# Retention scores contracted in two halves of 64 rows, into two PSUM banks, with spread queries of half the size

## The chip, the cores and the metric

One core of one Trainium2 chip runs the kernel. The time is that of one execution on the device in microseconds, the median of three runs. Before the change it is 919.24 us (918.93 to 920.19).

## The reference, cut to what matters

The program takes x of 4 batches, 1024 positions and 128 channels, normalizes it, and adds two branches to it: a block with retention, and a network of two layers of local attention (8 heads of 64, windows of 64) with a gated feed-forward part. The change concerns the retention alone. It has 16 heads of 8 channels, and a decay for each head:

```python
q = l2_normalize(xn @ qw.T)
k = l2_normalize(xn @ kw.T)
v = xn @ vw.T
dmask = jnp.where(causal[None], gammas[:, None, None] ** exponent[None], 0.0)
sim = jnp.einsum('bhnd,bhmd->bhnm', qh, kh) * scale
sim = sim * dmask[None]
yh = jnp.einsum('bhnm,bhmd->bhnd', sim, vh)
```

## The kernel before, in words

All tensors are fp32, but for a small mask. Positions are worked on in 8 tiles of 128 for all 4 batches. Each engine has a program of its own, written out in the order in which it issues; semaphores hold the engines together, and no planner moves anything. `run_bodies` goes through 16 steps of the attention (8 tiles by 2 layers); each step has four slots, one for each batch. In the eight steps of the first layer, a stage of retention for the same tile follows the last slot: `pe_retention`, `dve_retention` and `pool_retention`, each with the four batches as blocks b = 0 to 3. So there are 8 such stages and 32 blocks, and they lie in the first half of the execution.

Inside a block the 128 positions are 4 chunks (c, NBL) of 32. The decays are put on the queries and keys (aqk), so that the mask of a chunk's scores is only causal. The 128 channels are 16 heads of 8; a head is 4 g + j, with a group g (0 to 3, 32 channels each) and a place j in the group. The queries are spread over the groups: `qx` (in the memory of `prT`) holds for each chunk four copies of the turned queries, copy g with all channels but those of group g set to zero (`group_mask`, GpSimd, L528). The keys are spread over the places in the same manner (`kx`, VectorE, L1030). The steps on TensorE:

- `pe_block_scores` (L1722): for each chunk one matmul, keys `kx` as weights (128 rows, 128 columns: place and key), queries `qx` as moving data (128 columns: group and query). Result: a quarter of `score_bank(b)`, one of the two banks of pQK.
- VectorE multiplies it by the causal mask into `sm` (`dve_block_scores`, L1064).
- `pe_block_sums` (L1686) sums keys times values of each chunk, 32 columns of the array for each group, and VectorE makes `before`, the sums before each chunk (L1038).
- `pe_block_output` writes into pY (one bank, the groups on different 32 partitions): the carried state times the queries (L1696, 4 matmuls of 32 weight columns and 128 moving ones), the sums before the chunk times the queries (L1702, 12 of 32 by 32), and, once `vx` and `sm` are there, values times masked scores (L1709, 16 of 32 by 32).

The remaining names: L1628 projects a batch, L1637 turns queries and keys, L1675 spreads values, L1449 and L1451 transpose for the layer norm of the step before (not in the first stage), L1274 and L1728 follow the stage. The first scores of a stage wait for VectorE's last product of slot 3 (`mul_done`, L867), since that reads pQK too. Before `pe_block_scores` writes its bank, it waits until the masked product of two blocks earlier is through (`need(eng, A["sm"], n - 1)`).

Of the kernel before, what the change touches and what calls it, by code (L numbers as in the profile page):

```python
# [12 lines left out]
P = 128  # L13
# [5 lines left out]
BL = 32  # L19
NBL = P // BL  # L20
NG = 4
DEPTH = 2
H, DH = 8, 64
INNER = H * DH
# [9 lines left out]
C_HM = C_CAUSAL + BL  # L34
C_GM, C_SD = C_HM + NG, C_HM + 2 * NG
C_END = C_SD + 1
# [3 lines left out]
def constants():  # L40

    f = np.float32
    cst = np.zeros((P, C_END), f)
    i = np.arange(P)
    cst[:, C_ID:C_ID + P] = np.eye(P)
    cst[:, C_GRP:C_GRP + P] = (i[:, None] // RD == i[None, :] // RD) / RD
    cst[:, C_CAUSAL:C_CAUSAL + BL] = i[:, None] % BL <= i[None, :BL]
    lin = np.linspace(np.log(1.0 / 32.0), np.log(1.0 / 512.0), RH).astype(f)
    gam = (f(1.0) - np.exp(lin)).astype(np.float64)
    head = i // RD  # L50
    cst[:, C_GQ:C_GQ + P] = gam[head][None, :] ** i[:, None] / np.sqrt(RD)
    cst[:, C_GK:C_GK + P] = gam[head][None, :] ** (-i[:, None].astype(np.float64))
    col_head = np.arange(BL) // RD
    same = (head[:, None] % NG == col_head[None, :]).astype(np.float64)
    decayed = same * (gam[head] ** P)[:, None]
    cst[:, C_BD:C_BD + P] = np.concatenate([same] * (NBL - 1) + [decayed], 1)
    cst[:, C_VM:C_VM + P] = i[:, None] // BL == head[None, :] % NG
    cst[:, C_HM:C_HM + NG] = head[:, None] % NG == np.arange(NG)[None, :]
    cst[:, C_GM:C_GM + NG] = head[:, None] // NG == np.arange(NG)[None, :]
    cst[:, C_SD] = gam[head] ** P  # L60

    half = np.arange(0, DH, 2, dtype=f)
    inv = (f(1.0) / np.power(f(10000.0), half / f(DH))).astype(f)
    t = np.arange(T, dtype=f)
    fr = t[:, None] * inv[None, :]
    fr = np.concatenate([fr, fr], -1)
    base = ((half + f(0.4 * DH)) / f(1.4 * DH)).astype(f)
    power = (t - f(T // 2)) / f(WIN // 2)
    sc = np.power(base[None, :], power[:, None]).astype(f)
    sc = np.concatenate([sc, sc], -1)  # L70
    sign = np.where(np.arange(DH) < DH // 2, -1.0, 1.0).astype(f)
    cos, sin = np.cos(fr), np.sin(fr) * sign
    tab = np.stack([cos * sc * f(8), cos / sc, sin * sc * f(8), sin / sc], 1).astype(f)
    tab = tab.reshape(NT, P, 4, DH).transpose(1, 0, 2, 3)

    own = (i[:WIN, None] >= i[None, :WIN])
    before = (i[:WIN, None] <= i[None, :WIN])
    first = np.concatenate([own, np.zeros_like(before)], 1)
    even = np.concatenate([own, before], 1)
    odd = np.concatenate([before, own], 1)  # L80
    mask = np.where(np.concatenate([first, even, odd], 1), 0.0, MASKED).astype(f)
    mask = np.concatenate([mask, np.eye(WIN, dtype=f)], 1)
    mask = np.concatenate([mask, mask], 0)
    return cst, np.ascontiguousarray(tab), np.ascontiguousarray(mask)


def need(eng, sem, value):

    if isinstance(value, int) and value <= 0:
        return  # L90
    eng.wait_ge(sem, value)


def program(nc, a, out):
    with ExitStack() as ctx:
# [7 lines left out]
        cst = sb("cst", [P, C_END])  # L103
        ident = cst[:, C_ID:C_ID + P]
        group_avg = cst[:, C_GRP:C_GRP + P]
        causal = cst[:, C_CAUSAL:C_CAUSAL + BL]
        decay_q = cst[:, C_GQ:C_GQ + P]
        decay_k = cst[:, C_GK:C_GK + P]
        same_head = cst[:, C_BD:C_BD + P].rearrange("p (c n) -> p c n", c=NBL)
        value_mask = cst[:, C_VM:C_VM + BL].rearrange("p (h d) -> p h d", h=NG)  # L110
        place_mask = cst[:, C_HM:C_HM + NG]
        group_mask = cst[:, C_GM:C_GM + NG]
        state_decay = cst[:, C_SD:C_SD + 1]
        hidden = sb("hidden", [P, NC * NB * P])
        mask32 = hidden[:, 0:MASK_END]
# [1 line left out]
        tab = sb("tab", [P, NT, 4, DH])  # L117
        gain = sb("gain", [P, DEPTH, 2, DH])
        rope = [sb("rope0", [P, NT, 4, DH]), tab]
        warm = sb("warm", [P, 3])  # L120
        half_neg = sb("half_neg", [P, NB * NT])
        wqkv = sb("wqkv", [P, DEPTH, 3 * INNER])
        wo = sb("wo", [P, DEPTH, 4, D])
        w1 = sb("w1", [P, DEPTH, 2 * HID])
        w2 = sb("w2", [P, DEPTH, NC, D])
        b1c = sb("b1c", [P, DEPTH, 2, NC])
        b1e = sb("b1e", [P, DEPTH, 2, NC])
# [34 lines left out]
        m1 = sb("m1", [P, 2, 2 * INNER])  # L162
# [9 lines left out]
        prT = sb("prT", [P, H, P])  # L172
# [23 lines left out]
        state = sb("state", [P, NB, BL])  # L196

        vx = sb("vx", [P, 2, NBL, P])
        kx = hidden[:, 0:2 * INNER].rearrange("p (u c j n) -> p u c j n", u=2, c=NBL, j=NG)
        qx = prT[:, :, :].rearrange("p h n -> p (h n)").rearrange("p (u c g n) -> p u c g n", u=2, c=NBL, g=NG)  # L200
        sm = m1[:, 0, :].rearrange("p (u c g n) -> p u c g n", u=2, c=NBL, g=NG)
        before = sb("before", [P, NB, NBL, BL])
        ayT = gg[:, 0, :]
        afh = avm[:, :, :, :].rearrange("p u c n -> p u (c n)")
# [6 lines left out]
        pQK = ctx.enter_context(nc.psum_tensor("pQK", [P, 1024], F32))  # L211
# [8 lines left out]
        pY = pS[:, 512:1024]  # L220
# [3 lines left out]

            return pM if b else pT

        def score_bank(b):

            return pQK[:, 512 * (b % 2):512 * (b % 2) + 512]


        x_ld = [sem(f"x_ld{b}") for b in range(NB)]
# [18 lines left out]
        A = {n: sem(f"a_{n}") for n in (  # L251
            "xa", "qkv_mm", "sqq", "v", "floor", "rs", "qk", "t_mm", "t_ev", "vx_mm", "vx", "kx", "qx", "st_mm", "sm",
            "kv_mm", "kvm", "y_mm", "yt", "faded", "state", "ow_mm", "x1", "cs")}
# [266 lines left out]
        def pool_place_queries(eng, t, b):  # L520

            n = 4 * t + b
            shape = [P, NBL, NG, BL]
            eng.wait_ge(A["t_ev"], n + 1)
            if b == 0:
                eng.wait_ge(LS["o_mm"], count((0, t), 0) + 1)
            need(eng, A["y_mm"], n - 1)
            eng.tensor_tensor(qx[:, b % 2, :, :, :],  # L528
                              aqkT[:, b % 2, 0, :].rearrange("p (c n) -> p c n", c=NBL).unsqueeze(2).broadcast_to(shape),
                              group_mask.unsqueeze(1).unsqueeze(3).broadcast_to(shape), ALU.mult).then_inc(A["qx"], 1)  # L530
# [529 lines left out]
        def dve_block_scores(eng, t, b):  # L1060
            n = 4 * t + b
            eng.wait_ge(A["st_mm"], n + 1)
            need(eng, A["y_mm"], n - 1)
            eng.tensor_tensor(sm[:, b % 2, :, :, :],  # L1064
                              score_bank(b).rearrange("p (c g n) -> p c g n", c=NBL, g=NG),
                              causal.unsqueeze(1).unsqueeze(1).broadcast_to([P, NBL, NG, BL]),
                              ALU.mult).then_inc(A["sm"], 1)

        def dve_retention_out(eng, t):
# [620 lines left out]
        def pe_block_output(eng, t, b):  # L1690

            n = 4 * t + b
            need(eng, A["state"], t)
            for g in range(NG):
                rows = slice(BL * g, BL * g + BL)
                eng.matmul(pY[rows, b * P:(b + 1) * P].rearrange("p (c n) -> p c n", c=NBL), state[:, b, :],  # L1696
                           qx[:, b % 2, :, g, :], start=True, stop=False, skip_group_check=True)
            eng.wait_ge(A["kvm"], n + 1)
            for c_ in range(1, NBL):
                for g in range(NG):  # L1700
                    rows, col0 = slice(BL * g, BL * g + BL), b * P + c_ * BL
                    eng.matmul(pY[rows, col0:col0 + BL], before[:, b, c_ - 1, :], qx[:, b % 2, c_, g, :], start=False,  # L1702
                               stop=False, skip_group_check=True)
            eng.wait_ge(A["vx"], n + 1)
            eng.wait_ge(A["sm"], n + 1)
            for c_ in range(NBL):
                for g in range(NG):
                    rows, col0 = slice(BL * g, BL * g + BL), b * P + c_ * BL
                    mm = eng.matmul(pY[rows, col0:col0 + BL], vx[:, b % 2, c_, rows], sm[:, b % 2, c_, g, :],  # L1709
                                    start=False, stop=True, skip_group_check=True)  # L1710
            mm.then_inc(A["y_mm"], 1)

        def pe_block_scores(eng, t, b):

            n = 4 * t + b
            if b == 0:
                eng.wait_ge(LS["mul_done"], 8 * t + 8)
            eng.wait_ge(A["kx"], n + 1)
            eng.wait_ge(A["qx"], n + 1)
            need(eng, A["sm"], n - 1)  # L1720
            for c_ in range(NBL):
                mm = eng.matmul(score_bank(b)[:, c_ * P:(c_ + 1) * P], kx[:, b % 2, c_, :, :], qx[:, b % 2, c_, :, :],  # L1722
                                start=True, stop=True)
            mm.then_inc(A["st_mm"], 1)

        def pe_retention_out(eng, t):
# [85 lines left out]
```

## Time and profile before

| | |
|---|---|
| median of 3 runs | 919.24 us |
| profiled execution | 919.0 us, of which 917.2 us span |
| granted TensorE clock, mean | 0.992 of full speed |
| TensorE matmuls busy | 859.2 us |
| TensorE weight loads busy | 585.2 us |
| VectorE / ScalarE / GpSimd busy | 647.3 / 556.1 / 599.6 us |
| scores, L1722, inside their stages | 35.6 us in 256 records |
| GpSimd's spread of queries, L528 | 32 of 1040 ns |

The span is the time from the first to the last recorded instruction; the execution's own time has 1.8 us around it. PE is TensorE's matmuls, PEld its weight loads, DVE VectorE, ACT ScalarE, POOL GpSimd. An entry such as 64*128 after the names is the number of rows and columns of the array that the instruction uses. Matmuls overlap, and a record's duration holds the way through the array, so that the distance from start to start tells more than a duration.

### The profile page before, as it was taken

How to read it: one execution, taken by the hardware profiler on the slowest of the kernel's cores; microseconds unless marked ns; L12 is line 12 of the kernel's file. 1: busy time of each engine (PE TensorE's matmuls, PEld its weight loads, DVE VectorE, ACT ScalarE, POOL GpSimd, SP SyncE). 2: the span in 40 equal slices, each digit the busy share in tenths (PEclk: the TensorE clock that was granted, in tenths of full speed). 3: DMA queues.
4: the chain of work that ended last, by engine and by line, in shares of the span. 5: the costliest groups of instructions: out<-in, count | busy, mean ns of one | idle time of the engine just before them, and what ended most of it. 6: DMA issues, size and time to landing. Idle time of an engine off the chain costs nothing.

```text
span 917.2 us, 26458 instructions
## 1 busy us (share of the span) xinstructions
PE 859.2 (94%) x10918; PEld 585.2 (64%) x10918; DVE 647.3 (71%) x1119; ACT 556.1 (61%) x1109; POOL 599.6 (65%) x471
## 2 busy tenths in 40 slices
PE   1778999999999999999999989999999999999998
PEld 0446675776757767577676656666665757575756
DVE  4886766867767767677686776768585858685854
ACT  0365565766657567566676547575757575766663
POOL 4585758866676667666585664858585767667641
PEclk9899999999999999999999999999999999999999
DMA  9310211202112111020120211213131312131201
GB/s 297 72 39 19 46 23 33 51 18 41 30 21 56 21 30 42 17 53 17 36 48 16 44 40 27 55 27 76 27 80 24 79 25 73 32 73 25 53 1 36
DMA packets 127811, 41.82 MB, mean 46 GB/s; under 512 B 103715, under 2 KB 126925, under 8 KB 127565
## 3 DMA queue, kind: packets, MB, share of 16 engines
q1 hardware_dynamic: 122516, 38.82, 18.8%
q10 hardware_dynamic: 5177, 1.31, 0.7%
q8 instruction: 88, 1.44, 0.7%
q14 instruction: 30, 0.25, 0.1%
HBM read 9.70 MB, written 2.10 MB: 13 GB/s over the span
## 4 chain that ended last, share of the span: by engine, by line
PE 70%; DVE 16%; issue 6%; ACT 5%; POOL 2%; DMA 1%; SPq 0%; POOLq 0%; DVEq 0%; ACTq 0%
PE pQK L1405 9%; PE pT L1274 6%; PE pS L1333 6%; PE pT L1317 5%; PE pS L1306 5%; PE pV L1372 5%; DVE m L867 4%; PE pM L1489 4%; PE pM L1351 4%; PE pQK L1722 4%; PE pT L1467 3%; DVE hn L993 2%; PE pS L1293 2%; PE pM L1345 2%; PE pV L1351 2%
## 5 line engine op out<-in xcount | busy, mean ns | idle before, releaser
L463 POOL TENSOR_TENSOR rn<-rn,half_neg 128x16 f32<-128x16 f32 x64 | 187.4, 2929 | 5.3
L476 POOL TENSOR_TENSOR m<-m 128x1024 f32<-128x1024 f32 x64 | 150.8, 2356 | 0.1
L1405 PE MATMUL pQK<-wqkv,hT 128*128 128x512 f32 x256 | 123.0, 603 | 5.7 <-DVE m L867 5.7
L483 POOL TENSOR_TENSOR qkn<-m,rn 128x1024 f32<-128x1024 f32 x64 | 121.7, 1902 | 4.4
L461 POOL TENSOR_SCALAR rn<-ss 128x16 f32<-128x16 f32 x64 | 16.3, 254 | 158.4 <-DVE ss L910 157.1
L918 DVE TENSOR_REDUCE mx<-pS 128x8 f32<-128x1024 f32 x64 | 77.9, 1217 | 55.1 <-PE pS L1306 55.0
L687 ACT ACTIVATE prT<-pT 128x1024 f32<-128x1024 f32 x64 | 65.5, 1024 | 67.9 <-PE pT L1317 67.7
L650 ACT ACTIVATE sq<-pQK 128x1024 f32<-128x1024 f32 x64 | 65.4, 1022 | 35.2 <-PE pQK L1405 35.0
L681 ACT ACTIVATE kT<-pT 128x512 f32<-128x512 f32 x64 | 38.2, 597 | 72.2 <-PE pT L1274 72.2
L910 DVE TENSOR_REDUCE ss<-sq 128x16 f32<-128x1024 f32 x64 | 77.5, 1212 | 4.7 <-ACT sq L650 4.6
L722 ACT ACTIVATE pr<-pr 128x1024 f32<-128x1024 f32 x64 | 67.3, 1052 | 22.2 <-DVE pr L920 22.2
L920 DVE TENSOR_TENSOR pr<-pS,mx 128x1024 f32<-128x1024 f32 x64 | 78.4, 1225 | 2.2
L867 DVE TENSOR_TENSOR m<-pQK,rope 128x1024 f32<-128x1024 f32 x64 | 76.3, 1216 | 0.0
L867 DVE TENSOR_TENSOR m<-pQK,tab 128x1024 f32<-128x1024 f32 x64 | 76.2, 1212 | 0.0
L1333 PEld LDWEIGHTS pS<-vmix,prT 128*64 128x64 f32 x1024 | 64.5, 137 | 18.4 <-issue 13.8
L1274 PE MATMUL pT<-cst,qkn 128*128 128x128 f32 x512 | 69.5, 279 | 4.3 <-issue 3.4
L1333 PE MATMUL pS<-vmix,prT 128*64 128x65 f32 x1024 | 73.3, 225 | 0.0
L1333 PE MATMUL pS<-vown,prT 128*64 128x65 f32 x1024 | 73.3, 225 | 0.0
L1372 PE MATMUL pV<-wqkv,hT 128*128 128x512 f32 x128 | 67.3, 608 | 5.7 <-DVE gst L1169 2.7
L1405 PEld LDWEIGHTS pQK<-wqkv,hT 128*128 128x128 f32 x256 | 44.8, 192 | 41.4 <-issue 31.6
L1317 PE MATMUL pT<-cst,pr 128*128 128x128 f32 x512 | 70.0, 280 | 0.0
L1306 PE MATMUL pS<-kT,qT 64*64 64x128 f32 x2048 | 67.9, 271 | 0.0
(228 smaller groups left out, 1855.1 us busy)
## 6 DMA issues: line engine op xcount, KB each, us to landing
vmix<-vown SPq DMA_DIRECT2D x124, 128.0 KB, 2.8
kT<-kT SPq DMA_DIRECT2D x60, 128.0 KB, 2.7
x<-in_L_attn_x SPq DMA_DIRECT2D x4, 512.0 KB, 9.6
hT<-xnT SPq DMA_DIRECT2D x64, 32.0 KB, 1.9
xs<-in_L_attn_x SPq DMA_DIRECT2D x8, 256.0 KB, 3.1
hT<-x2T SPq DMA_DIRECT2D x64, 32.0 KB, 1.9
out<-aqkT SPq DMA_DIRECT2D x7, 256.0 KB, 2.2
wqkv<-in_L_ffn_wqkv SPq DMA_DIRECT2D x2, 768.0 KB, 10.0
```

The costliest lines, as they stand in the source:

```text
L463: eng.tensor_tensor(rn[:, k % 2, :], rn[:, k % 2, :], half_neg[:, 0:2 * H], ALU.pow).then_inc(S["rn_done"], 1)
L476: eng.tensor_tensor(m1[:, k % 2, :], m1[:, k % 2, :], m2[:, :], ALU.add).then_inc(S["add_done"], 1)
L483: eng.tensor_tensor(qkn[:, k % 2, :].rearrange("p (h d) -> p h d", d=DH), m1[:, k % 2, :].rearrange("p (h d) -> p h d", d=DH), rn[:, k % 2 ...
L867: eng.tensor_tensor(m.rearrange(shape, g=2, h=H, **sizes), src, by, ALU.mult).then_inc(S["mul_done"], 1)
L918: eng.tensor_reduce(mx[:, :], sc, AX.X, ALU.max).then_inc(S["mx_done"], 1)
L920: eng.tensor_tensor(pr[:, b % 2, :, :], sc, mx[:, :].unsqueeze(2).broadcast_to([P, H, P]), ALU.subtract).then_inc(S["sub_done"], 1)
L1274: mm = eng.transpose(pT[:, j * P:(j + 1) * P], qkn[:, b % 2, j * P:(j + 1) * P], ident)
L1306: mm = eng.matmul(pS[64 * w:64 * w + 64, col0:col0 + P], qT[r, j, 64 * w:64 * w + 64], keys, start=False, stop=True, skip_group_check=True)
L1317: mm = eng.transpose(pT[:, j * P:(j + 1) * P], pr[:, b % 2, j, :], ident)
L1333: mm = eng.matmul(pS[64 * w:64 * w + 64, col0:col0 + DH + 1], prT[:, i, 64 * w:64 * w + 64], (vown if w else vmix)[b][:, 2 * j + g, :], st ...
L1372: eng.matmul(pV[:, :], hT[:, k, :], wqkv[:, l, 1024:1536], start=True, stop=True).then_inc(S["v_mm"], 1)
L1405: mm = eng.matmul(pQK[:, g * 512:(g + 1) * 512], hT[:, k, :], wqkv[:, l, g * 512:(g + 1) * 512], start=True, stop=True)
```

## The change

The queries are spread over two copies in place of four: in each half of the partitions (64 channels, two groups) copy 0 holds the first group of that half and copy 1 the second. The scores of a chunk are then two matmuls, one for each half of 64 rows, with 64 moving columns each; half r goes to bank r of pQK, where block b takes the part b % 2. The masked product reads both banks, and `sm` has the half as a further index. The state and the sums before the chunk are multiplied with the half of rows that the group lies in. The wait ahead of the scores asks for the product of the block before.

```diff
-    cst[:, C_GM:C_GM + NG] = head[:, None] // NG == np.arange(NG)[None, :]
+    cst[:, C_GM:C_GM + NR] = head[:, None] // NG % NR == np.arange(NR)[None, :]
...
-        qx = prT[:, :, :].rearrange("p h n -> p (h n)").rearrange("p (u c g n) -> p u c g n", u=2, c=NBL, g=NG)
-        sm = m1[:, 0, :].rearrange("p (u c g n) -> p u c g n", u=2, c=NBL, g=NG)
+        qx = prT[:, 0:4, :].rearrange("p h n -> p (h n)").rearrange("p (u c g n) -> p u c g n", u=2, c=NBL, g=NR)
+        sm = m1[:, 0, :].rearrange("p (u r c g n) -> p u r c g n", u=2, r=2, c=NBL, g=NR)
...
-        def score_bank(b):
-
-            return pQK[:, 512 * (b % 2):512 * (b % 2) + 512]
+        def score_half(b, r):
+
+            return pQK[:, 512 * r + 256 * (b % 2):512 * r + 256 * (b % 2) + 256]
...
-            shape = [P, NBL, NG, BL]
+            shape = [P, NBL, NR, BL]
...
-            eng.tensor_tensor(sm[:, b % 2, :, :, :],
-                              score_bank(b).rearrange("p (c g n) -> p c g n", c=NBL, g=NG),
-                              causal.unsqueeze(1).unsqueeze(1).broadcast_to([P, NBL, NG, BL]),
+            eng.tensor_tensor(sm[:, b % 2, :, :, :, :].rearrange("p r c g n -> p r (c g) n"),
+                              pQK[:, :].rearrange("p (r u z n) -> p u r z n", r=2, u=2, n=BL)[:, b % 2, :, :, :],
+                              causal.unsqueeze(1).unsqueeze(1).broadcast_to([P, 2, NBL * NR, BL]),
                               ALU.mult).then_inc(A["sm"], 1)
...
             for g in range(NG):
-                rows = slice(BL * g, BL * g + BL)
-                eng.matmul(pY[rows, b * P:(b + 1) * P].rearrange("p (c n) -> p c n", c=NBL), state[:, b, :],
-                           qx[:, b % 2, :, g, :], start=True, stop=False, skip_group_check=True)
+                rows, half = slice(BL * g, BL * g + BL), slice(64 * (g // NR), 64 * (g // NR) + 64)
+                eng.matmul(pY[rows, b * P:(b + 1) * P].rearrange("p (c n) -> p c n", c=NBL), state[half, b, :],
+                           qx[half, b % 2, :, g % NR, :], start=True, stop=False, skip_group_check=True)
...
-                    eng.matmul(pY[rows, col0:col0 + BL], before[:, b, c_ - 1, :], qx[:, b % 2, c_, g, :], start=False,
-                               stop=False, skip_group_check=True)
+                    eng.matmul(pY[rows, col0:col0 + BL], before[half, b, c_ - 1, :], qx[half, b % 2, c_, g % NR, :],
+                               start=False, stop=False, skip_group_check=True)
...
-                    mm = eng.matmul(pY[rows, col0:col0 + BL], vx[:, b % 2, c_, rows], sm[:, b % 2, c_, g, :],
+                    mm = eng.matmul(pY[rows, col0:col0 + BL], vx[:, b % 2, c_, rows], sm[:, b % 2, g // NR, c_, g % NR, :],
                                     start=False, stop=True, skip_group_check=True)
...
-            need(eng, A["sm"], n - 1)
+            need(eng, A["sm"], n)
             for c_ in range(NBL):
-                mm = eng.matmul(score_bank(b)[:, c_ * P:(c_ + 1) * P], kx[:, b % 2, c_, :, :], qx[:, b % 2, c_, :, :],
-                                start=True, stop=True)
+                for r in range(2):
+                    rows = slice(64 * r, 64 * r + 64)
+                    mm = eng.matmul(score_half(b, r)[:, c_ * 64:(c_ + 1) * 64], kx[rows, b % 2, c_, :, :],
+                                    qx[rows, b % 2, c_, :, :], start=True, stop=True)
             mm.then_inc(A["st_mm"], 1)
```

## Rows read from the trace of the kernel before

**Rows 1.** The page's busy times: us, share of the span, instructions.

```profile
PE 859.2 (94%) x10918; PEld 585.2 (64%) x10918; DVE 647.3 (71%) x1119; ACT 556.1 (61%) x1109; POOL 599.6 (65%) x471
```

**Rows 2.** The page's chain that ended last, by engine and by line.

```profile
PE 70%; DVE 16%; issue 6%; ACT 5%; POOL 2%; DMA 1%; SPq 0%; POOLq 0%; DVEq 0%; ACTq 0%
PE pQK L1405 9%; PE pT L1274 6%; PE pS L1333 6%; PE pT L1317 5%; PE pS L1306 5%; PE pV L1372 5%; DVE m L867 4%; PE pM L1489 4%; PE pM L1351 4%; PE pQK L1722 4%; PE pT L1467 3%; DVE hn L993 2%; PE pS L1293 2%; PE pM L1345 2%; PE pV L1351 2%
```

**Rows 3.** The chain in order of time: start us, us, what; pieces of three stages.

```profile
131.58 1.09 issue
...
239.08 1.14 DVE m L867
...
240.27 1.16 PE pQK L1722 x8
...
252.53 0.19 PE pS L1702 x24
...
427.74 0.16 issue
```

**Rows 4.** TensorE's timeline, fourth stage: start us, us, engine, line, operation, tile, records.

```profile
240.27 1.16 PE L1722 MATMUL pQK<-prT,hidden 128*128 128x128 f32 x8 [0.23 <-DVE m L867]
241.36 0.42 PE L1686 MATMUL pS<-avm,aqk 128*32 128x128 f32 x8
241.71 0.44 PE L1637 MATMUL pM<-cst,aqk 128*128 128x128 f32 x2
242.08 0.46 PE L1675 MATMUL pT<-aT,xa 128*32 128x32 f32 x32
242.47 0.91 PE L1628 MATMUL pT<-aT,xa 128*128 128x384 f32 x2
...
244.38 0.44 PE L1637 MATMUL pM<-cst,aqk 128*128 128x128 f32 x2
244.66 1.06 PE L1722 MATMUL pQK<-prT,hidden 128*128 128x128 f32 x8
245.64 0.46 PE L1675 MATMUL pT<-aT,xa 128*32 128x32 f32 x32
245.92 0.45 PE L1686 MATMUL pS<-avm,aqk 128*32 128x128 f32 x8
246.14 0.44 PE L1696 MATMUL pS<-prT,state 128*32 128x128 f32 x8
246.36 0.41 PE L1702 MATMUL pS<-prT,before 128*32 128x32 f32 x24
246.79 0.46 PE L1709 MATMUL pS<-m,vx 128*32 128x32 f32 x32
...
250.19 1.16 PE L1722 MATMUL pQK<-prT,hidden 128*128 128x128 f32 x8
251.19 0.60 PE L1449 MATMUL pM<-cst,xr 128*128 128x128 f32 x4
251.72 0.46 PE L1451 MATMUL pM<-cst,xr 64*128 64x64 f32 x4
252.10 0.42 PE L1696 MATMUL pS<-prT,state 128*32 128x128 f32 x8
```

**Rows 5.** TensorE's weight loads in the timeline, at three places.

```profile
35.24 2.36 PEld L1763 LDWEIGHTS pM<-col,w 128*128 128x128 f32 x23 [0.24 <-issue]
...
222.64 1.01 PEld L1306 LDWEIGHTS pS<-kT,qT 64*64 64x64 f32 x32
...
251.71 0.32 PEld L1451 LDWEIGHTS pM<-cst,xr 64*128 64x128 f32 x4 [0.17 <-issue]
```

**Rows 6.** VectorE's timeline, and GpSimd's products by line (ns min/median/max).

```profile
245.36 0.69 DVE L1030 TENSOR_TENSOR hidden<-pM,cst 128x512 f32<-128x512 f32 x1 [1.17 <-ACT aqkT L760]
245.97 0.68 DVE L1064 TENSOR_TENSOR m<-pQK,cst 128x512 f32<-128x512 f32 x1
...
L515 POOL TENSOR_TENSOR state<-state,cst x8: 398/398/402, 86.2 to 500.0; 128x128 f32<-128x128 f32 x8
L528 POOL TENSOR_TENSOR prT<-aqkT,cst x32: 1039/1040/1042, 66.5 to 485.7; 128x512 f32<-128x512 f32 x32
```

More of the change, by code:

```diff
@@ L21 @@
 NG = 4
+NR = 2
 DEPTH = 2
@@ L111, in program @@
         place_mask = cst[:, C_HM:C_HM + NG]
-        group_mask = cst[:, C_GM:C_GM + NG]
+        group_mask = cst[:, C_GM:C_GM + NR]
         state_decay = cst[:, C_SD:C_SD + 1]
@@ L1700, in pe_block_output @@
                 for g in range(NG):
-                    rows, col0 = slice(BL * g, BL * g + BL), b * P + c_ * BL
-                    eng.matmul(pY[rows, col0:col0 + BL], before[:, b, c_ - 1, :], qx[:, b % 2, c_, g, :], start=False,
-                               stop=False, skip_group_check=True)
+                    rows, half = slice(BL * g, BL * g + BL), slice(64 * (g // NR), 64 * (g // NR) + 64)
+                    col0 = b * P + c_ * BL
+                    eng.matmul(pY[rows, col0:col0 + BL], before[half, b, c_ - 1, :], qx[half, b % 2, c_, g % NR, :],
+                               start=False, stop=False, skip_group_check=True)
             eng.wait_ge(A["vx"], n + 1)
```

## The prediction

> **What bounds the kernel now.** The busy times of the page come first: TensorE is busy for 94% of the span and the others for 61 to 71% [rows 1]. The chain that ended last says the same by its shares: 70% of it is TensorE, and the scores of line 1722, which the change rewrites, are 4% [rows 2]. The share is an average, so I read the chain through one retention stage, 240 to 254 us, the fourth of eight [rows 3]. There a VectorE product (L867) releases the first scores, and from then until the output projection the chain is TensorE, without VectorE, ScalarE or GpSimd in it. What TensorE loses in these 14 us goes into the span; what another engine gains there does not. The exceptions are idle pieces, which the chain names "issue": I counted 11 in six of the eight stages, 0.16 to 1.09 us each, 4.96 us in all; the largest and the smallest stand in [rows 3]. In them TensorE waits for nothing recorded in the middle of a stream of small matmuls.
>
> Then the timeline of TensorE in the same stage, from one group's start to the next [rows 4]. A tiling is the rows by columns of the array that a matmul takes. The scores take 0.98 us (244.66 to 245.64) if the group before them has their tiling, 128*128, and the one after has not; 1.00 us (250.19 to 251.19) the other way round; and 1.09 us (240.27 to 241.36) if both differ. So entering with a new tiling costs the scores 0.11 us and leaving for another costs 0.09. The same is seen elsewhere: L1637 lasts 0.37 us ahead of L1675 and 0.28 ahead of L1722 (exit 0.09); L1675 lasts 0.39 us ahead of L1628 and 0.28 ahead of L1686, which has its tiling (exit 0.11); L1686 lasts 0.35 us between other tilings and 0.22 between equal ones (entry and exit 0.13). That this also holds where only the rows change is shown by L1449 to L1451, 128*128 to 64*128: the four L1451 matmuls take 0.38 us, though their loads step by (0.32 - 0.14)/3 = 0.06 us [rows 4, 5], so 0.14 us of it is entry and exit.
>
> **The scores themselves.** 4 matmuls of 128 moving columns become 8 of 64 on 64 rows each. Each fp32 matmul leaves two load and matmul records, so 8 steps of 0.11 us become 16 records on two halves of the array. What a step costs is the larger of load and matmul. The loads at L1763, whose matmuls move one column, show the load alone: 23 of them, two thirds with 128 columns and a third with 85, take 2.36 us [rows 5]; less the last one's 0.16 that is 22 steps of 0.10 us, or 0.11 us for 128 columns. So the old step was bounded by the load as much as by the matmul, and the new weights still have 128 columns. Halving the moving columns gains nothing. The two halves can load side by side: at L1306, with two row and two column halves, 32 loads of 133 ns start every (1.01 - 0.13)/31 = 0.03 us [rows 5]. So 8 steps of 0.11 us remain: 0 gained. Bounds: -0.40 us a block if a step falls to the 0.06 of L1451, +0.89 if the halves load one after the other. I take 0, because the load at L1763 has the same type and width.
>
> The Trainium skill (TensorEngine Tiling (Array Packing), Theoretical Speedup) gives up to 2x for a contraction of 64 rows or fewer. By it the scores would halve, 32 x 0.44 = 14 us less; the loads at L1763 speak against it, and it is the first rival below.
>
> **The new changes of tiling**, per stage of four blocks, old order kept:
> - Scores 1 and 2 follow the transposes of L1637, until now in one tiling: exit 0.09 plus entry 0.11, twice: 0.40 us.
> - Scores 0, 1 and 2 leave for 128*32 as before, but the last matmul moves 64 columns and not 128, and drains 0.05 us sooner: -0.15.
> - Scores 3 to the layer norm's transposes (L1449) were one tiling: exit 0.04 beyond a 0.11 step, entry 0.05: 0.09 (not in the first stage, which has no such transposes).
> - The state matmuls (L1696) become 64*32. For blocks 0 to 2 they follow L1686 (128*32): entry and exit 0.13, three times: 0.39. Block 3 changed tiling there already.
> - From L1702 (now 64*32) to L1709 (still 128*32), in all four blocks, 0.13 each (the exit of L1675, 0.11, and an entry of 0.02): 0.52.
> Together 1.25 us a stage, 10.0 in eight, 9.9 without the first stage's missing transposes. No 64*32 matmul stands in the trace; a price of nothing for a change in rows alone at 32 columns would take 0.91 away, and I keep 0.13 since L1451 shows the row change at 128 columns.
>
> The matmuls of L1696 and L1702 stay as many, with the same moving columns and four column places: 0. If the two row halves could not write the shared bank pY together, a block would lose what its column parallelism gives twofold: 0.22 (L1696, [rows 4]) and 0.19 (L1702, [rows 3]), 0.41 us. Below zero nothing can come, since four run together already. The Trainium skill (PSUM — Partial Sum Buffer, PSUM bank collisions raise a hardware error) says different row tiles may not access one bank at once, and in another sentence that quadrants are apart; here the halves write different quadrants, and no row shows such a pair.
>
> **What swallows part of it.** Block 1's masking product (L1064) ends at 245.97 + 0.68 = 246.65 us, and L1709 waits for it: L1702 to L1709 lasts 0.43 us, not the 0.19 of [rows 3]. It began when VectorE came free from L1030, not when the scores were ready (245.7) [rows 4, 6]. Before this point TensorE is now 0.7 us later and the product some 0.2 us: the wait of 0.24 us goes, in seven of eight stages: -1.7. The idle pieces shrink if they are late instructions, because TensorE asks for fewer per us; but the scores bring 16 more records a block, 512 in all. Between 0 and -4 us I take -1.3, a quarter of the 4.96.
>
> **Costed at nothing.** GpSimd's spread of the queries (L528) has 256 elements for 512: by 1040 ns for 512 and 398 for 128 [rows 6] it takes about 0.61 us, 0.43 less in 32 places, 13.8 us of GpSimd time. The first lies under VectorE's L867, which ends at 240.22 and releases the scores [rows 3]; the others end a microsecond before their scores. Uncovered, it would be worth up to those 13.8 us. The masking product reads two banks in place of one, but the same 512 elements from PSUM: 0.68 us; twice that would be seen in block 1 alone. The wait for A["sm"] asks for one more: n. Scores b stand behind output b - 1 in TensorE's order, which has waited for that same product, so it has always been met; were it not, everything of TensorE behind it would wait 0.68 us.
>
> **Sum.** 9.9 - 1.7 - 1.3 = 6.9 us on the profiled execution's 919.0 us (span 917.2, 1.8 around it). That execution lies 0.2 under the median of 919.24, so I forecast 926.0.
>
> **Rivals.**
> 1. The loads of a half are cheaper. Steps of 0.06 us give 32 x 0.40 = 12.8 us back: 926.0 - 12.8 = 913. For it: L1451's steps. Against it: those are transposes, and the fp32 loads at L1763 need twice that. It decides for a gain as soon as a step falls below 0.083 us (6.9/256 under 0.11). Chance 8%.
> 2. A change of rows alone at 32 columns costs nothing. Only the scores' 0.34 us a stage remain, 2.7 us, of which the wait in block 1 takes some 1.2: 920.5, no measurable change. For it: no such pair is in the trace. Against it: L1449 to L1451. Chance 10%.
> 3. The halves exclude each other: in pY, 32 x 0.41 = 13 us more, 939; in the loads, 32 x 0.89 = 28 us more, 954. Against it: L1306. Chance 7%.
>
> **How the numbers follow.** The forecast has 75%, and its own range is 923 to 931: the idle pieces absorbing 0 or 4 us, and a change priced 0.10 to 0.17. A measurement of this kernel tells 0.2%, 1.8 us, from no change. Faster is rival 1 and a rest: 9%. The same is most of rival 2 and a rest: 11%. Slower is 80%. The range, 920.5 to 934, leaves out rivals 1 and 3 and a little below.
>
> **What would show it.** In the timeline of TensorE: scores of 16 records that last 1.0 to 1.1 us in all four blocks (0.6 would be rival 1, 1.9 the serial loads); turns (L1637) of 0.37 us ahead of scores 1 and 2; about 0.35 us for L1686 in every block and 0.31 for L1702 (0.22 and 0.19 would be rival 2; L1696 of 0.45, rival 3); GpSimd's spread at 0.6 us and a stage 0.8 to 1.2 us longer. The forecast is wrong if the scores get shorter, or if TensorE's stage grows and the span does not.

## The result: 925.5 us, 0.59% slower

The changed kernel takes 925.5 us (median of five) against 919.24 for the kernel before; the ratio, 1.0059 [1.0038, 1.008], goes by four of the five (923.19, 924.6, 925.5 and 927.73, of which the median is 925.05). The fifth, 1103.75 us, ran at a lower granted clock (0.757 against 0.99). The forecast was 926.0, with a range of 920.5 to 934.

The profiled execution of the changed kernel is 923.19 us (span 921.4, granted clock 0.990), 4.2 us over its partner's 919.0. Here are its busy times, and the shares of its chain that ended last by engine and by line; they answer to [rows 1] and [rows 2].

```profile
PE 866.0 (94%) x11174; PEld 585.0 (63%) x11174; DVE 648.3 (70%) x1119; ACT 555.5 (60%) x1109; POOL 586.0 (64%) x471
```

```profile
PE 70%; DVE 15%; issue 5%; ACT 5%; POOL 3%; DMA 1%; SPq 0%; POOLq 0%; DVEq 0%; ACTq 0%
PE pQK L1406 9%; PE pT L1275 6%; PE pT L1318 6%; PE pS L1334 6%; PE pS L1307 5%; PE pV L1373 5%; PE pM L1490 4%; PE pM L1352 4%; PE pQK L1726 4%; DVE m L868 4%; PE pT L1468 3%; DVE hn L994 2%; PE pS L1294 2%; PE pM L1346 2%; PE pV L1352 2%
```

TensorE is busier by 6.8 us, with 256 more matmul records (two for each of 128 more matmuls); GpSimd is less busy by 13.6; the other two have moved by a microsecond or less. The loads' busy time has not grown either, though there are 256 more of them: two halves load side by side, and in the scores the matmul records of the two halves start 6 or 7 ns apart. The lines lie one down (L1406 is the old L1405, L1318 the old L1317), up to four down past the state matmuls: L1687, L1697, L1704, L1711 and L1726 answer to L1686, L1696, L1702, L1709 and L1722.

TensorE's timeline of the fourth stage answers to [rows 4]. Columns: start, length, engine, line, operation, tile in rows*columns, the shapes, the records, and what ended an idle time before them.

```profile
239.61 1.11 PE L1726 MATMUL pQK<-prT,hidden 64*128 64x64 f32 x16 [0.23 <-DVE m L868]
240.65 0.43 PE L1687 MATMUL pS<-avm,aqk 128*32 128x128 f32 x8
241.01 0.44 PE L1638 MATMUL pM<-cst,aqk 128*128 128x128 f32 x2
241.37 0.46 PE L1676 MATMUL pT<-aT,xa 128*32 128x32 f32 x32
241.76 0.91 PE L1629 MATMUL pT<-aT,xa 128*128 128x384 f32 x2
...
243.89 0.44 PE L1638 MATMUL pM<-cst,aqk 128*128 128x128 f32 x2
244.26 1.11 PE L1726 MATMUL pQK<-prT,hidden 64*128 64x64 f32 x16
245.29 0.46 PE L1676 MATMUL pT<-aT,xa 128*32 128x32 f32 x32
245.57 0.45 PE L1687 MATMUL pS<-avm,aqk 128*32 128x128 f32 x8
245.95 0.42 PE L1697 MATMUL pS<-prT,state 64*32 64x128 f32 x8
246.19 0.37 PE L1704 MATMUL pS<-prT,before 64*32 64x32 f32 x24
246.49 0.46 PE L1711 MATMUL pS<-m,vx 128*32 128x32 f32 x32
...
250.21 1.11 PE L1726 MATMUL pQK<-prT,hidden 64*128 64x64 f32 x16
251.25 0.66 PE L1450 MATMUL pM<-cst,xr 128*128 128x128 f32 x4
251.84 0.46 PE L1452 MATMUL pM<-cst,xr 64*128 64x64 f32 x4
252.23 0.42 PE L1697 MATMUL pS<-prT,state 64*32 64x128 f32 x8
```

Read it by the starts, as in the prediction: the length of a row is modelled and runs into the next group, the difference of two starts is what a group costs. Two rows of the changed kernel by line (least, median and greatest ns, then when) stand beside [rows 6]:

```profile
L529 POOL TENSOR_TENSOR prT<-aqkT,cst x32: 612/612/614, 64.9 to 489.3; 128x256 f32<-128x256 f32 x32
L1065 DVE TENSOR_TENSOR m<-pQK,cst x32: 681/691/693, 67.9 to 493.0; 128x512 f32<-128x512 f32 x32
```

For each group of a stage I took its shortest step over the seven full stages of a trace. Their sum is the **array time** of a stage, what it would last if TensorE never stalled and waited no longer than in its best stage. The stage is measured from its first scores to its output projection, eight of them in a trace.

| | before | after |
|---|---|---|
| array time of a stage, us | 12.95 | 14.09 |
| stalls in the middle of small matmuls, us in all | 7.2 (11) | 5.4 (9) |
| eight stages, us | 113.25 | 119.05 |

A stall is a step of over 0.2 us between two matmuls of one group that is no regular one (those of the scores are up to 0.22), counted with its whole step; in the prediction these were the idle pieces, where the chain's "issue" counts only the idle part. The time outside the stages is the same (between two stages 39.4 or 45.2 us, tail 425.7), but the first scores of this execution started at 66.17 us and before's at 67.78. So of 5.8 us in the stages only 4.2 appear in the profiled pair; the medians, 6.3 apart, agree better with the stages.

### The profile page after: what moved, and what is told of

It reads as the page before. It is cut to its first block, busy times and chain, and to the rows that moved or that the text cites. A ratio compares the mean times of both kernels' runs of the same rounds, so it can differ in the third digit from the quotient of the medians.

```text
span 921.4 us, 26970 instructions
## 1 busy us (share of the span) xinstructions
PE 866.0 (94%) x11174; PEld 585.0 (63%) x11174; DVE 648.3 (70%) x1119; ACT 555.5 (60%) x1109; POOL 586.0 (64%) x471
## 4 chain that ended last, share of the span: by engine, by line
PE 70%; DVE 15%; issue 5%; ACT 5%; POOL 3%; DMA 1%; SPq 0%; POOLq 0%; DVEq 0%; ACTq 0%
PE pQK L1406 9%; PE pT L1275 6%; PE pT L1318 6%; PE pS L1334 6%; PE pS L1307 5%; PE pV L1373 5%; PE pM L1490 4%; PE pM L1352 4%; PE pQK L1726 4%; DVE m L868 4%; PE pT L1468 3%; DVE hn L994 2%; PE pS L1294 2%; PE pM L1346 2%; PE pV L1352 2%
## 5 line engine op out<-in xcount | busy, mean ns | idle before, releaser
L1406 PE MATMUL pQK<-wqkv,hT 128*128 128x512 f32 x256 | 123.2, 604 | 5.1 <-DVE m L868 5.1
L1318 PE MATMUL pT<-cst,pr 128*128 128x128 f32 x512 | 70.8, 282 | 0.0
L1406 PEld LDWEIGHTS pQK<-wqkv,hT 128*128 128x128 f32 x256 | 44.8, 192 | 40.8 <-issue 31.8
```

The source lines that it names most:

```text
L1318: mm = eng.transpose(pT[:, j * P:(j + 1) * P], pr[:, b % 2, j, :], ident)
L1406: mm = eng.matmul(pQK[:, g * 512:(g + 1) * 512], hT[:, k, :], wqkv[:, l, g * 512:(g + 1) * 512], start=True, stop=True)
```

## The experiments

Times are medians beside the kernel before's on the same chip: 918.43 us for the first four, 920.04 for the next four, 920.10 for the last four. "After" in an edit is the changed kernel.

### Which half of the change costs

**e1_scores_only: scores in halves, state and sums as before** (four copies of the queries again, so the spread is full size).

```diff
-                    mm = eng.matmul(score_bank(b)[:, c_ * P:(c_ + 1) * P], kx[:, b % 2, c_, :, :], qx[:, b % 2, c_, :, :],
+                    mm = eng.matmul(score_half(b, r)[:, c_ * 64:(c_ + 1) * 64], kx[rows, b % 2, c_, :, :],
+                                    qx[rows, b % 2, c_, 2 * r:2 * r + 2, :], start=True, stop=True)
```

> The kernel before with the scores' part of the change alone: two matmuls of 64 rows a chunk into two banks, but queries spread over four copies and state and sums multiplied on all 128 rows. Theory (changes of tiling): scores of 1.04 us in every block (0.98, 0.98, 1.00 and 1.09 before), the turns ahead of scores 1 and 2 at 0.37 us, L1702 at 0.19; a stage 0.3 us longer, 2.7 us in all, of which idle pieces and the wait of block 1 may take half: 920.5 to 922. Rival (the whole loss is from the scores, by their 512 added records): 925, as the full change.

Measured: 924.87 us, +6.4, ratio 1.0080 [1.0052, 1.0107]. The steps came out as expected, the time did not: it is the rival's 925. TensorE's timeline:

```profile
246.62 1.11 PE L1726 MATMUL pQK<-prT,hidden 64*128 64x64 f32 x16
247.66 0.46 PE L1676 MATMUL pT<-aT,xa 128*32 128x32 f32 x32
...
248.38 0.41 PE L1704 MATMUL pS<-prT,before 128*32 128x32 f32 x24
...
251.67 0.27 PE L1687 MATMUL pS<-avm,aqk 128*32 128x128 f32 x1 [0.48 <-issue]
...
255.84 0.45 PE L1711 MATMUL pS<-m,vx 128*32 128x32 f32 x28 [0.47 <-issue]
```

The scores take 1.04 us, and the array time of a stage grew by some 0.35 to 0.4 us, 3 us in all. The rest is in the last two rows: groups cut in the middle, with nothing waited for. The stalls went from 7.2 to 10.4 us (12 of them). The expected figure had let them shrink.

**e2_outputs_only: state and sums on half rows, scores as before.**

```diff
-                eng.matmul(pY[rows, b * P:(b + 1) * P].rearrange("p (c n) -> p c n", c=NBL), state[:, b, :],
-                           qx[:, b % 2, :, g, :], start=True, stop=False, skip_group_check=True)
+                eng.matmul(pY[rows, b * P:(b + 1) * P].rearrange("p (c n) -> p c n", c=NBL), state[half, b, :],
+                           qx[half, b % 2, :, g, :], start=True, stop=False, skip_group_check=True)
```

and `before[half, ...]`, `qx[half, ...]` in the same way.

> The kernel before with the other part alone: state and sums before the chunk multiplied on the 64 rows of their group's half, the scores and the spread of before. Theory (a change of rows alone drains, at 32 columns too): L1686 at 0.35 us in every block, L1702 at 0.30, seven changes of 0.13 us a stage, 7.3 us in all, less 1 to 3 in idle pieces: 923 to 925. Rival (only the scores' tiling costs): 919.2, no change. With the scores-only kernel the two differences should add up to the full change's 6 us within 1.5.

Measured: 921.03 us, +2.6, 1.0024 [1.0007, 1.0042], under the 923 to 925 expected. TensorE's timeline of a block:

```profile
247.51 0.45 PE L1686 MATMUL pS<-avm,aqk 128*32 128x128 f32 x8
247.88 0.42 PE L1696 MATMUL pS<-prT,state 64*32 64x128 f32 x8
248.13 0.37 PE L1703 MATMUL pS<-prT,before 64*32 64x32 f32 x24
248.43 0.46 PE L1710 MATMUL pS<-m,vx 128*32 128x32 f32 x32
```

L1686 takes 0.37 us, not 0.22, and L1703 takes 0.30, not 0.19: a change of rows alone drains the array at 32 columns too, and the second rival falls. The Trainium skill (TensorEngine Tiling (Array Packing), Key Properties) says that a change of the tiling mode drains TensorE; the trace agrees and adds the price. L1696 with two halves writing one bank takes 0.25 us, so nothing excludes anything there. The array time grew by 0.79 us a stage, 0.85 if the 0.06 us of waiting in the shortest step of before's block 1 is left out, 6.8 in all. The waits ahead of L1710 shrank by 2.5 us (1.8 of them in block 1, the rest in blocks 2 and 3, which I had not counted) and the stalls by 1.5. That leaves 2.8: the eight stages of the trace are 2.7 longer, the median 2.6.

**e3_full_spread: the changed kernel, with the queries spread at full size.**

```diff
-            shape = [P, NBL, NR, BL]
+            shape = [P, NBL, NG, BL]
```

with the mask and `qx` as before, and g for g % NR.

> The changed kernel with the queries spread over four copies again (GpSimd's product 1.04 us in place of 0.61), its matmuls as changed. Theory (the spread lies under other work): the time of the changed kernel, 925.5, within 1 us. Rival (GpSimd's saving pays part of the loss back, up to 13.8 us): 927 or more.

Measured: 925.64 us, +7.2, 1.0081 [1.0061, 1.0101]; the changed kernel has 1.0059 [1.0038, 1.008]. The intervals overlap, and the eight stages of the two traces differ by 0.6 us (119.6 and 119.05): GpSimd's 13.6 us are worth nothing that can be told from noise. e1 and e2 cost 6.4 and 2.6 us, together 9.0 against 7.2 for both at once (e3); that they would add up to 6 within 1.5 us was missed. Array times add up (0.35 to 0.4 and 0.79 make the 1.14 of the table); stalls do not.

### What bounds a step of the scores

**e4_half_moving: the kernel before, with half of the moving columns of the scores.**

```diff
-                mm = eng.matmul(score_bank(b)[:, c_ * P:(c_ + 1) * P], kx[:, b % 2, c_, :, :], qx[:, b % 2, c_, :, :],
+                mm = eng.matmul(score_bank(b)[:, c_ * P:c_ * P + 64], kx[:, b % 2, c_, :, :], qx[:, b % 2, c_, 0:2, :],
```

> The kernel before with the scores' matmuls moving 64 of their 128 columns (two of the four groups' queries; the rest of the scores is left out), weights and tiling as before. Theory (a step of the scores is bounded by the load of 128 fp32 weight columns, 0.11 us): scores still 0.98 us in the timeline, 0.05 less at the exit, 918 to 919. Rival (the step is bounded by what moves): steps of 0.06 us, 0.45 us a block less, 32 times: 905 to 908, or 910 if idle pieces grow.

Measured: 918.75 us, +0.3, 1.0005 [0.9988, 1.0022].

```profile
246.09 1.00 PE L1722 MATMUL pQK<-prT,hidden 128*128 128x64 f32 x8
247.03 0.46 PE L1675 MATMUL pT<-aT,xa 128*32 128x32 f32 x32
```

From start to start 0.94 us, against 0.98 in [rows 4]. Only the exit got shorter, by the 0.05 us of 64 columns that need not drain. The step stays at 0.11 us: the load of 128 weight columns sets it. The Trainium skill (TensorEngine Tiling (Array Packing), Theoretical Speedup) gives up to 2x for contractions of at most 64 rows; here two row tiles gave none, 1.04 us for 0.98.

**e5_narrow_weights: the changed kernel, with half of the weight columns of the scores.**

```diff
-                    mm = eng.matmul(score_half(b, r)[:, c_ * 64:(c_ + 1) * 64], kx[rows, b % 2, c_, :, :],
+                    mm = eng.matmul(score_half(b, r)[0:64, c_ * 64:(c_ + 1) * 64], kx[rows, b % 2, c_, 0:2, :],
```

> The changed kernel with 64 of the 128 weight columns in the scores' matmuls (two of the four places' keys; the rest of the scores is left out); as many records as in the change. Theory 1 (the load bounds the step): steps of 0.06 us, the scores 0.55 us in place of 1.04, 2 us a stage less of array time. Theory 2 (TensorE cannot take more than 256 records in some 3.7 to 4 us, stretch after stretch; all idle pieces so far stand at every 256th record): most of that comes back as idle pieces, which grow from 5.4 us to over 12, and the time is 914 to 919. Rival (idle pieces are chance and stay): 925.5 - 16 = 909.5 or less.

Measured: 922.12 us, +2.1, 1.0019 [1.0005, 1.0032].

```profile
244.96 0.68 PE L1726 MATMUL pQK<-prT,hidden 64*64 64x64 f32 x16
245.57 0.46 PE L1676 MATMUL pT<-aT,xa 128*32 128x32 f32 x32
...
249.81 0.38 PE L1687 MATMUL pS<-avm,aqk 128*32 128x128 f32 x2 [0.89 <-issue]
```

The scores fall to 0.61 us: that the load bounds them is shown from the other side. Inside the group the step halved: by the starts of the records, the pairs of the two halves follow each other every 0.059 us, against 0.112 in the changed kernel; what is left of the 0.61 is the first step and the exit. Block 0 keeps 0.84 us, because the group after it now waits for VectorE (this trace's waits, in the columns explained below):

```profile
PE pS L1687 <- DVE o L931: 1.3, 8, 0.2
```

The array time fell by 1.24 us a stage, 9.9 in all, and not by the 2 us a stage that were expected; the 922.12 us lie above all that was expected, and by the ratios the kernel is only 3.7 us faster than the changed one. Where the rest went shows in the waits. Each row here is of another trace, the changed kernel's, e1's and this one's, over the stages: the line that waited and what for, us in all, times, the longest.

```profile
PE pS L1711 <- issue: 3.1, 5, 0.9
```

```profile
PE pS L1711 <- issue: 6.4, 9, 1.0
```

```profile
PE pS L1711 <- issue: 6.9, 7, 1.3
```

The stalls of all groups are 5.4, 10.4 and 11.8 us. Less array time, or more records in the same time, and the stalls give part of it back.

### Reordering the projections

Every change of tiling costs, so I tried to save two by putting the projection of block 3 ahead of the values of block 1.

```diff
-                    pe_block_values(eng, t, 1)
                     pe_retention_project(eng, t, 3)
+                    pe_block_values(eng, t, 1)
```

**e6_before_project_early** does it in the kernel before.

> The kernel before with the projection of batch 3 (L1628) moved ahead of the values of block 1 (L1675), so that it follows the turn in the same tiling: two changes of tiling fewer a stage. Theory: the array's time for a stage 0.3 us shorter, 2.6 us in all; where the 256-record limit is met it comes back as idle pieces: 917 to 918.5. Rival (changes of tiling are free when nothing else differs): 919.

**e7_after_project_early** does it in the changed kernel.

> The same move in the changed kernel. Theory: 0.3 us a stage less array time, part of it back as idle pieces: 923.5 to 925, still slower than the kernel before. Rival: 925.5.

Measured: 923.6 us, +3.6, 1.0030 [1.0016, 1.0044], and 927.17, +7.1, 1.0078 [1.0053, 1.0104]. Both missed. In e6 the groups that change their order take 0.33 us less as expected, but the wait of L1709 in block 1 grew: L1702 to L1709 lasts 1.37 us, for 0.43 before (in e7 0.81, for 0.30). A first guess, that the stalls had only moved to worse places, was put to e10 below.

### The stalls stand at every 256th record

In every trace the stalls stand at one place in a count. Count the records of TensorE (loads, matmuls and waits) from its first, which is 1: each stall of the stages (127 in the 14 traces) comes at 238 or 239 modulo 256, whatever the line there; not every such count has one. Here are two in the chain of the changed kernel's seventh stage (start, length, engine and line, matmuls):

```profile
426.93 0.30 PE pS L1711 x19
427.23 0.54 issue
427.77 0.32 PE pS L1711 x13
...
430.69 0.33 PE pS L1711 x24
431.01 0.94 issue
431.95 0.27 PE pS L1711 x8
```

The ends of the two stalls are 4.18 us apart (431.95 - 427.77), the time that 256 records then took. The 43 stretches of 256 that have a stall at both ends took 3.5 to 4.8 us, 3.9 at the median. TensorE gets through the small matmuls faster than that: stretches of the stages without a stall at their end took as little as 2.6 us.

What TensorE runs out of can be read from the same traces. The page lists one DMA queue for instructions that grows with TensorE's records; here are the kernel before and the changed one (packets, MB, share):

```profile
q8 instruction: 88, 1.44, 0.7%
```

```profile
q8 instruction: 90, 1.47, 0.7%
```

Each packet has 16384 bytes, and TensorE has 22571 and 23083 records: 256 records for a packet. The packets' times lie in the trace's DMA records. For the two stalls above they are 425.14 to 426.35 and 429.10 to 430.53 us: TensorE goes on 1.42 us after each has landed. Call the counts 256 n + 238 marks, each with the n-th packet. In all 127 stalls TensorE goes on 1.17 to 1.62 us after the packet of the mark has landed, and at none of the 1232 marks of the 14 traces does it pass sooner than 1.17 us after that. So the stalls are late instructions: the 4.18 us are 1.33 from the last mark to the start of the next packet, 1.43 for the packet and 1.42 until TensorE goes on.

The experiments below rest on the count alone. If the stalls stand at it, waits that are met at once, put in long before the stages, must move the stalls to other matmuls and leave the array time alone.

**e8_before_shifted_128: 128 more waits in the kernel before,** after the first transposes.

```diff
                 mm.then_inc(awt_mm, 1)
+                for _ in range(128):
+                    eng.wait_ge(cst_ld, 32)
```

> The kernel before with 128 waits that are already met on TensorE after its first transposes, where it stands idle for 8.7 us; everything behind is the same, but 128 records later. Theory (idle pieces stand where TensorE passes a multiple of 256 records): the pieces are again at the same count within 256 and so at other matmuls than before; the time within 2 us of 919.2, either way, plus up to 1 us if the waits outlast the idle time. Rival (pieces belong to certain matmuls or to transfers at that time): the same pieces at the same lines, 128 records further in the count.

Measured: **915.54 us, -4.5, 0.9955 [0.9936, 0.9974].** That is more than the 2 us expected either way. The 128 waits left 64 records in the trace (the first load of the scores went from count 556 to 620). The stalls stand at 239 again, so at other matmuls, and only four are left, 3.1 us; each ends 1.46 to 1.60 us after its packet has landed. The array time is still 12.9. The largest one, in the chain:

```profile
304.85 0.21 PE pS L1709 x17
305.06 1.15 issue
306.21 0.32 PE pS L1709 x12
```

**e9_after_shifted_128** does the same in the changed kernel.

> The changed kernel, all of it 128 TensorE records later by waits that are already met, as in the shifted kernel before. Theory: the array's time for a stage stays 1.1 to 1.2 us above that of the kernel before whatever the place; idle pieces at the 256-record marks fall elsewhere, in all 2 to 8 us: 922 to 928, and 6 to 10 above the kernel before at the same shift (915.5), which had few pieces left to shrink. Rival (the change's 6 us are the place of the marks): within 2 us of 915.5.

Measured: 922.08 us, +2.0, 1.0025 [1.0004, 1.0046]; array time 14.1, stalls 3.1 us. It is 6.5 us over e8.

**e10_project_early_shifted_128** is e6's order with the same 128 waits.

> The kernel before with batch 3's projection moved ahead (which lost 3.6 us) and shifted by 128 records. Theory (the loss was the place of the marks, which this move changes against the work around them): the loss shrinks or turns, 912 to 917. Rival (the move itself costs, by a later wait in block 1): 3 us above the shifted kernel before, 918.5 or more.

Measured: 921.57 us, +1.5, 1.0024 [1.0008, 1.0041], 6.0 us over e8, with stalls of 6.9 us. The guess about e6 falls, the rival holds, and more stalls come on top. TensorE's, ScalarE's and VectorE's timelines:

```profile
188.13 0.41 PE L1702 MATMUL pS<-prT,before 128*32 128x32 f32 x24
189.50 0.46 PE L1709 MATMUL pS<-m,vx 128*32 128x32 f32 x32 [0.96 <-DVE m L1064]
```

```profile
185.35 1.11 ACT L769 ACTIVATE vx<-pT 32x128 f32<-32x128 f32 x4 [0.51 <-PE pT L1675]
...
187.78 0.25 ACT L760 ACTIVATE aqkT<-pM 128x128 f32<-128x128 f32 x1
```

```profile
188.06 0.69 DVE L1030 TENSOR_TENSOR hidden<-pM,cst 128x512 f32<-128x512 f32 x1 [1.79 <-ACT aqkT L760]
188.67 0.68 DVE L1064 TENSOR_TENSOR m<-pQK,cst 128x512 f32<-128x512 f32 x1
```

With the values of block 1 later, ScalarE copies them (1.11 us) later and turns to the keys of block 2 later; VectorE has them first in its order and reaches the masking product some 0.9 us later. TensorE then waits 0.96 us for it, more than the two changes of tiling had cost.

**e11_before_shifted_64** and **e12_after_shifted_64** shift by half as much (64 waits, 32 records).

> The kernel before shifted by 64 records. Theory: stages keep 12.95 us of array time, and the time moves with the sum of idle pieces alone, one us for one us, somewhere in 914 to 922. Rival (the shift of 128 gained by something else, such as the start): 915.5 again.

> The changed kernel shifted by 64 records. Theory: 922 to 928, and above the kernel before at that shift by 9.4 us less what its idle pieces have fewer than that kernel's. Rival: the same time as the kernel before at that shift.

Measured: 917.36 us, -2.7, 0.9974 [0.9952, 0.9996], stalls 5.3 us; and 922.39 us, +2.3, 1.0019 [1.0003, 1.0034], stalls 3.1 us. The expected distance between the two was 9.4 less the 2.3 of the stalls, 7.1 us; it is 5.0, because that sum left out the waits ahead of L1709, which fall from 3.3 to 0.5 us. All six together:

| records ahead | before, us (stalls) | after, us (stalls) | difference |
|---|---|---|---|
| 0 | 919.24 (7.2) | 925.5 (5.4) | 6.3 |
| 32 | 917.36 (5.3) | 922.39 (3.1) | 5.0 |
| 64 | 915.54 (3.1) | 922.08 (3.1) | 6.5 |

The stalls are those of one profiled execution each. The change costs 5.0 to 6.5 us at the three placements (4.1 to 6.4 by the ratios). In the profiled stages alone it costs 5.8, 4.5 and 6.7 us. e8, the kernel before with 64 records more, is the fastest version of all, and beats both kernels.

## Why the prediction was right

The mechanism and its sum held. Point by point, each term from the shortest steps:

- **TensorE bounds the stages.** Right: e3 takes GpSimd's saving away and nothing moves that can be told from noise.
- **The scores themselves, 0 gained.** Right: 1.04 us in all four blocks (predicted 1.0 to 1.1), and e4 and e5 show that the load is the bound. Rival 1 would have given 0.6 us. That a step bounded by less would be 0.06 us was borne out too: e5, with 64 weight columns, has 0.059.
- **Scores 1 and 2, entry 0.20 and exit -0.05.** Right: 0.99 before, 1.04 after, and the turns ahead of them 0.27 before and 0.37 after, so +0.15 us a block.
- **Scores 3 to the layer norm, 0.09.** 0.10 measured, with the turn's steps at L1450 (0.53 before, 0.59 after).
- **Into the state matmuls, 3 x 0.13 = 0.39.** 0.49 measured: L1687 went from 0.24, 0.22 and 0.22 to 0.36, 0.38 and 0.38, and L1697 from 0.22 to 0.24.
- **L1702 to L1709, 4 x 0.13 = 0.52.** This one was too large: 0.30 to 0.37 measured. L1704 is 0.30 us in all blocks (0.19 before without a wait), +0.11, and L1711 takes 0.39 where it had mostly taken 0.42. The exit came as taken from L1675, the entry of 0.02 did not, and I did not expect the next group to come out 0.03 us shorter. Why it does is open.
- **Sum of the changes of tiling, 1.25 a stage.** 1.14 by the shortest steps; the shortest steps of before still held 0.06 us of block 1's wait, and without it 1.2, 9.6 us in all.
- **Block 1's wait, -1.7.** Right: 0.43 before, 0.30 after, like the other blocks, -1.8 in all; in e2, which leaves the scores alone, it went too. The sum had no term for the same waits in blocks 2 and 3, which gave 0.7 us more.
- **Stalls, -1.3.** 7.2 to 5.4 by whole steps, -1.8 in the profiled pair; the size was near by luck. That they are late instructions was right, as the packets of q8 show; that their number per us decides was incomplete. It is rather each stretch of 256 records: which matmuls its end falls on, and how dense the stretch was. At 32 and 64 records ahead the change moves the stalls by -2.3 and by nothing, so the -1.8 is of this placement, not of the change.
- **Halves that exclude each other (rival 3).** Refuted: L1697 has 0.24 us, not 0.45, and the loads do not queue. The Trainium skill (PSUM — Partial Sum Buffer, PSUM bank collisions raise a hardware error) forbids two row tiles in one bank and exempts quadrants. Here the two row halves write different quadrants of pY, and the trace agrees with the exemption: eight records in 0.24 us, for 0.22 in one row tile.
- **Costed at nothing.** The spread takes 612 ns (610 estimated) and is worth nothing; the product takes 691 ns at the median, for 681 before; in the changed kernel no wait for A["sm"] appears ahead of the scores.

The terms as measured, 9.6 - 2.5 - 1.8 = 5.3 us, stand beside 5.8 in the profiled stages and 6.3 between the medians; the forecast's last digit is off by one, since 919.24 and 6.9 make 926.1.

What failed was in the expectations of experiments. In e1 I added array time and let the stalls shrink, and the denser stream, by more records, ran into more of them. In e5 the stalls grew to nearly the size expected (11.8 us for over 12), but the array time fell by 1.24 us a stage and not 2, since block 0 came to wait for VectorE. In e2 and e12 the waits ahead of L1709 in blocks 2 and 3 were left out.

## What to carry to other kernels

Where fp32 weight loads of 128 columns are the bound, as here, a split of a matmul into row halves gives nothing, and each new change of tiling costs 0.1 to 0.2 us. Where the moving columns are the bound it may pay; no run here tried that. Price the neighbours of a rewritten matmul, from start to start, before the matmul itself. When a small change moves a kernel of dense small matmuls by 0.5%, shift its instructions by a few dozen records with waits that are met at once, and compare both kernels at several shifts: 64 records alone were worth 4.5 us here.

## What was not expected of the hardware

- In the retention stages TensorE stalls, in steps of 0.2 to 1.46 us, at the same count of its records modulo 256 (238 or 239) in all 14 traces. It waits there for a packet of 16384 bytes on the instruction queue q8, and goes on 1.17 to 1.62 us after it has landed; from stall to stall 256 records took 3.9 us at the median. Every execution here was recorded, so whether the recording makes these packets later stays open; none of the runs could tell.
- 64 records of nothing ahead of the work made the kernel 4.5 us faster, 0.9955 [0.9936, 0.9974]; before's three times, 919.24, 917.36 and 915.54 us, follow its stalls of 7.2, 5.3 and 3.1 us.
- A change in rows alone, 128 to 64 at 32 columns, costs 0.14 to 0.18 us going in (L1687 and L1697 together) and 0.08 to 0.11 coming out (L1704 and L1711), about as much as a change of both.
